# TensorE's share of two edge loops written as an engine loop, with buffer rings of four, eight and ten

## The reference

```python
# layer 0
edge_messages = relu(concat(x[dst], x[src], edge_attr, u[batch[dst]]) @ W1.T + b1)
aggregated    = segment_sum(edge_messages, dst)
x = layernorm(x + relu(concat(x, aggregated, u) @ W2.T + b2))
# layer 1
h          = relu(concat(x[row], x[col], edge_attr) @ msg_w1 + msg_b1)
messages   = h @ msg_w2 + msg_b2
aggregated = segment_sum(messages, col) / max(count, 1)
x = layernorm(x + (relu(concat(x, aggregated) @ upd_w1 + upd_b1) @ upd_w2 + upd_b2))
```

## Time and profile before

| | us |
|---|---|
| median of 3 runs | 4138.87 (4137.64 to 4140.2) |
| the profiled execution, its own time | 4140.49 |
| its span, first to last instruction | 4138.7 |
| first L615 of layer 0 to its last L598 | 98.28 to 2005.48 |
| first L615 of layer 1 to its last L598 | 2133.50 to 4044.41 |

### The profile page before, as it was taken

The page is one execution under the profiler, slowest core; times in us unless marked ns, Lnnn a source line. Parts: engine busy times, 40 slices in busy tenths (PEclk is TensorE's granted clock), DMA queues, the critical chain, the costliest instruction groups (busy, mean ns, idle before and its releaser), DMA issues. The chain is left out here.

```text
span 4138.7 us, 53825 instructions
## 1 busy us (share of the span) xinstructions
PE 3378.5 (82%) x16906; PEld 3171.1 (77%) x16906; DVE 1671.5 (40%) x3965; ACT 591.0 (14%) x1005; POOL 2981.5 (72%) x3156
## 2 busy tenths in 40 slices
PE   6998788877888888788779878878788787887886
PEld 4998787777878778787759877777777777777773
DVE  4544444444444444444445443434333333333333
ACT  1111111111111111111321111111111111111113
POOL 4777777777777777777267777777777777777772
PEclk6555555555555555555755555555555555555556
DMA  6554444444444444444155444444444444444431
GB/s 227 167 162 130 140 131 145 143 133 140 131 140 142 139 140 131 140 135 143 53 159 172 140 142 140 131 139 130 140 143 138 140 131 140 132 148 141 131 118 34
DMA packets 286577, 569.11 MB, mean 138 GB/s; under 512 B 165416, under 2 KB 197523, under 8 KB 248976
## 3 DMA queue, kind: packets, MB, share of 16 engines
q1 hardware_dynamic: 185326, 357.82, 25.7%
q0 software_dynamic: 100096, 205.20, 18.6%
q10 hardware_dynamic: 866, 2.56, 0.2%
HBM read 545.86 MB, written 19.45 MB: 137 GB/s over the span
## 5 line engine op out<-in xcount | busy, mean ns | idle before, releaser
L206 POOL DMA_INDIRECT Qr<-tabQ,srcE x3128 | 2960.7, 947 | 1074.7 <-issue 969.1
L615 PE MATMUL bank<-wall,BIG 128*128 128x128 f32 x6256 | 1596.3, 436 | 35.0 <-DMA BIG<-in_eaT 35.0
L628 PE MATMUL bank<-BIG 128*128 128x42 f32 x6256 | 1459.8, 413 | 13.0 <-ACT BIG L557 13.0
L615 PEld LDWEIGHTS bank<-wall,BIG 128*128 128x128 f32 x6256 | 1419.2, 331 | 35.4 <-DMA BIG<-in_eaT 35.4
L628 PEld LDWEIGHTS bank<-BIG 128*128 128x128 f32 x6256 | 1420.7, 331 | 13.6 <-ACT BIG L557 13.6
L587 DVE TENSOR_TENSOR BIG<-bank,Qr 128x512 f32<-128x512 f32 x782 | 539.6, 690 | 2097.9 <-issue 1727.3
L619 PE MATMUL bank<-BIG 126*128 126x128 bf16 x3128 | 484.1, 310 | 648.4 <-DVE BIG L570 647.8
L557 ACT ACTIVATE BIG<-BIG 128x512 f32<-128x512 f32 x782 | 492.4, 630 | 3364.1 <-DVE BIG L587 3364.1
L619 PEld LDWEIGHTS bank<-BIG 126*128 126x128 bf16 x3128 | 339.3, 141 | 774.8 <-DVE BIG L570 748.1
L570 DVE TENSOR_TENSOR BIG<-bank,BIG 126x512 bf16<-126x512 f32 x782 | 534.2, 683 | 34.3 <-DMA BIG<-in_dstR 34.0
L576 DVE TENSOR_TENSOR BIG<-bank,relE 128x168 f32<-128x168 f32 x782 | 251.5, 322 | 0.0
(11 more groups left out here) (94 smaller groups left out, 481.0 us busy)
## 6 DMA issues: line engine op xcount, KB each, us to landing
BIG<-in_eaT SPq DMA_DIRECT2D x196, 1024.0 KB, 5.6
BIG<-in_dstR SPq DMA_DIRECT2D x96, 1008.0 KB
Qr<-tabQ,srcE POOLq DMA_INDIRECT x3128, 2.5
BIG<-tabP SPq DMA_DIRECT2D x782, 31.5 KB
tabP<-BIG SPq DMA_DIRECT2D x24, 384.0 KB, 2.8
tabQ<-BIG SPq DMA_DIRECT2D x24, 256.0 KB, 4.0
X<-in_xN SPq DMA_DIRECT2D x1, 3136.0 KB, 12.0
out<-BIG SPq DMA_DIRECT2D x12, 256.0 KB, 2.3
```

What stands on the lines that cost most here:

```text
L206: e.indirect_dma_start(Q[:, g % R_Q, j, :], None, tabQ[l][:, :], bass.IndirectOffsetOnAxis(ap=srcE[:, g, j:j + 1], axis=0)).then_inc(es[l] ...
L615: e.matmul(bank[i % R_C][:, j * D:(j + 1) * D], ea[:, k % R_EA, (i % LQ * J + j) * P:(i % LQ * J + j + 1) * P], wc[l], start=(j == 0), sto ...
L628: last = e.matmul(bank[4 + g % 2][:, 0:W], M[:, g % R_M, j, :], S[:, g % R_S, j, :], start=(j == 0), stop=(j == J - 1))
```

## The change

TensorE's body becomes a function `group(i, t, dt)`. The first eight groups are written out as before, then a loop on the engine runs 47 turns of eight groups (groups 8 to 383) with the loop's register `t` from 1 to 47, and the last seven groups and the two trailing half turns are written out again. Inside the loop the slots of the rings are constants, so each ring that TensorE touches has to divide eight: `R_ST` goes from 3 to 4, `R_S` from 6 to 8, `R_M` from 3 to 4. Each wait's value is computed from `t`. `R_Q` goes from 12 to 10, and `PF`, which was `R_Q - 2`, is now `R_Q`, so that it stays 10. `BIG`, the area that holds the rings other than Q, grows from 11904 to 13072 words a partition. The other engines' code is unchanged but for the sizes of the rings.

```diff
-R_EA, R_PB, R_BC, R_Q, R_ST, R_S, R_M, R_PT = 2, 4, 2, 12, 3, 6, 3, 4
+R_EA, R_PB, R_BC, R_Q, R_ST, R_S, R_M, R_PT = 2, 4, 2, 10, 4, 8, 4, 4
+STEP = 8
-PF = R_Q - 2
-NBIG = 11904
+PF = R_Q
+NBIG = 13072
...
-                        for i in range(NG + 2):
-                            if i < NG:
+                        def group(i, t, dt):
+                            if dt + i < NG:
                                 k = i // LQ
                                 if i % LQ == 0:
-                                    e.wait_ge(v_ea[k % R_EA], 16 * (k // R_EA + 1))
-                                if i >= R_C:
-                                    e.wait_ge(v_tt, i - R_C + 1)
+                                    e.wait_ge(v_ea[k % R_EA], t * (16 * STEP // LQ // R_EA) + 16 * (k // R_EA + 1))
+                                if dt + i >= R_C:
+                                    e.wait_ge(v_tt, t * STEP + (i - R_C + 1))
...
-                                e.wait_ge(v_st, i + 1)
-                                e.wait_ge(v_pb[i % R_PB], 16 * (i // R_PB + 1))
+                                e.wait_ge(v_st, t * STEP + (i + 1))
+                                e.wait_ge(v_pb[i % R_PB], t * (16 * STEP // R_PB) + 16 * (i // R_PB + 1))
...
-                            if g >= 0:
-                                e.wait_ge(v_rl, g + 1)
-                                e.wait_ge(v_s, g + 1)
-                                if g >= 2:
-                                    e.wait_ge(v_ag, g - 1)
+                            if dt + g >= 0:
+                                e.wait_ge(v_rl, t * STEP + (g + 1))
+                                e.wait_ge(v_s, t * STEP + (g + 1))
+                                if dt + g >= 2:
+                                    e.wait_ge(v_ag, t * STEP + (g - 1))
...
-                                    e.wait_ge(v_cn, g + 1)
+                                    e.wait_ge(v_cn, t * STEP + (g + 1))
...
+                        for i in range(STEP):
+                            group(i, 0, 0)
+                        with e.Fori(1, NG // STEP) as t:
+                            for i in range(STEP):
+                                group(i, t, STEP)
+                        for i in range(NG // STEP * STEP, NG + 2):
+                            group(i, 0, 0)
```

## The result

The changed kernel takes 4154.81 us (median of 6 runs, 4152.76 to 4156.86) against 4138.77 us for the kernel before (6 runs, 4137.64 to 4141.1): 16.0 us more, a ratio of 1.0038 with a 95% interval of 1.0025 to 1.0051. The forecast was 17.6 us more.

A forecast was written before the change was run, and what follows sets the result against it. GpSimd's unbroken gathers were taken to bound both loops; 2 x (10.0 - 1.2) = 17.6 us added to the median of 4138.9 gave 4156.5 us, own range 4154 to 4160, eight in ten 4151 to 4168.

The forecast's parts named there:

- GpSimd bounds both loops: Both layers' loops: GpSimd's unbroken gathers need 5.00 us a group against TensorE's 4.02, so GpSimd sets each loop's end.
- Eight gathers per loop lose their head start: Start of each loop: with ten slots full, eight more gathers wait for the first sum, 10.0 us a loop, 20.0 together.
- The first load has less company: Start of each loop: without early gathers the first sum comes 1.2 us earlier, bounds 0 and 1.7.
- TensorE's loop costs nothing: TensorE's computed waits: 58 of 52 ns, 3.0 us a turn in layer 0, hidden by slack of 7.3 us a turn.
- The first rival: TensorE's loop: 165 ns exposed per computed wait makes TensorE the bound in layer 0, total 4274 us; chance 0.09.
- TensorE's waits on L570: Sign that the forecast is right: these waits of TensorE inside the loops shrink but stay.
- The body is fetched once: TensorE's jump back: fetching code anew costs nothing from below, 7.2 us a turn from above; nothing was taken.
- The rings of ST, S and M: Deeper rings let VectorE and ScalarE run further ahead inside the loops; price and gain nothing.
- The sum: Whole kernel: 17.6 us over the median of 4138.9, giving 4156.5 us, 0.43% slower.
- the second rival: Loops' gathers: GpSimd's step shrinks; 10 ns each gives 4126 us, faster than before from 5.8 ns on; chance 0.04.
- The two terms of the forecast: Loop starts: 10.0 us a loop for eight late gathers, less 1.2 us for an earlier first sum.

The follow-up runs named there:

- paced pair: Kernel before, and it with the changed rings, both taking two of four gathers plus memsets except in layer 0's first ring: 3976.20 and 3998.51 us.
- loop_q12: Changed kernel with Q's ring twelve instead of ten and S's ring four instead of eight: 5078.08 us, ratio 0.9993 to the kernel before; run again, 5139.51 us, 1.0066.
- loop_pf8: Changed kernel with eight instead of ten groups gathered ahead of each loop, Q's ring still ten: 5062.13 us, ratio 0.9966 to the kernel before.
- unrolled_rings: Kernel before with only the rings changed (Q ten with ten groups ahead, ST 4, S 8, M 4), TensorE's program unrolled: 5088.95 us, ratio 1.0011.
- half_loop: Changed kernel with only two of a group's four blocks of rows gathered from the eleventh group of each loop on: 3482.48 us.
- paced_before: Kernel before with two of four gathers replaced by three memsets each, in all groups but layer 0's first ring: 3976.20 us.
- half_unrolled: Changed kernel without TensorE's engine loop, only two of four blocks gathered from the eleventh group of each loop on: 3483.24 us.

## Why the prediction was right

- **GpSimd bounds both loops, at 5.00 us a group.** Right. After the change it waits on L588 at the two starts and otherwise keeps its gaps of 0.30, and the last gather of each loop carries the whole delay.
- **Eight gathers per loop lose their head start, 10.0 us each.** Right: the first gather of each loop ends a wait on the first sum, and the counts behind it are 1524. In the paced pair the same step gave two groups per loop, as worked out.
- **The first load has less company, 1.2 us a loop.** Right in kind and nearly in size: from the first load's issue to the first sum 1.36 us less in layer 0 and 1.04 in layer 1, bounds 0 and 1.7.
- **TensorE's loop costs nothing, at most 3.0 us a turn under the cover of its slack.** Right that it is nothing, and there is less to hide than I priced. I counted 58 computed waits of 52 ns; the values are shared, and the sequencer spends 0.5 us a turn on them and 0.2 on the jump. The cover was not even needed: with TensorE as the bound the pair differs by -0.8 us in 3482. The first rival falls. One sign of the forecast did not come: TensorE's waits on L570 (L571 now) were to shrink, from 647.8 us, and are 653.4 us (the weight loads' waits there did shrink, from 748.1 to 626.2).
- **The body is fetched once.** I left this between nothing and 7.2 us a turn. It is nothing: 18 blocks in all.
- **The rings of ST, S and M cost and gain nothing.** No row speaks against it; in the paced pair the loops are accounted for without them to 0.2 us, and the step inside them is the same.
- **The sum.** 17.6 us forecast, 16.0 measured; the loops of the profiled pair show 14.0. What the forecast did not have is a step of the gathers shorter by 1.4 ns in layer 0 and 0.8 ns in layer 1, 3.4 us in all. It goes the way of the second rival, at 1.1 ns on average a fifth of the 5.8 ns from which that would decide. It need not be the change's doing: one gather lasts 944 ns in the median in the changed kernel and 945 in the kernel before, but the same unrolled kernel with the changed rings shows 944, 944 and 947 on three chips, and `loop_q12` and `loop_pf8`, with TensorE's loop, 947. So an unrolled program, with all its code traffic, can have the shorter gather, and programs with the loop the longer one; what sets the two was not found. The two terms of the forecast come to 17.4 in the trace, 20.0 less 2.6 at the two starts; with the shorter step, 14.0 in the loops, and 12.3 for the whole spans. That the medians differ by 16.0, nearer to the forecast than the profiled pair does, is in part luck: the executions of either kernel scatter over 3.5 and 4.1 us.

## What to carry to other kernels

Find the engine that never waits, and ask of each edit what it does to the start of that engine's chain. A prefetch depth and a ring depth are two numbers. Here ten groups were gathered ahead in both kernels, and the ring alone, twelve or ten, set how many groups were under way when the first slot came free; taking memory from that ring to give it to others moved the end of each loop by whole steps. What the prefetch depth does to the time by itself no undisturbed run shows. An engine loop of 47 turns with some 340 matmul and load records a turn was free here even on a saturated TensorE, so its price was what it asked of the buffers.

## What the runs showed of the hardware

The same program took 4139 us on the first occasions and 5084 to 5109 us on the chips of the later ones, with the granted clock nearly the same (0.517 and 0.513) and the gather's step the same 1.25 us. There, while GpSimd issued gathers without a break, other engines stood still for 7 us (`unrolled_rings`, L598) to 24 us (`half_loop`, L181) at a time with no other engine's work outstanding, and in the stretch shown TensorE took 7.4 us for eight passes that take 2.06 otherwise. Halving the gathers, or spacing them with memsets, made it vanish from the loops (3482 and 3976 us, each kernel's runs within 8 us); ahead of the loops it stayed wherever the gathers stayed unbroken, and went in layer 1 of `paced_before`, where they were spaced. It is not the fetching of TensorE's code: the loop with its 18 blocks had it as much as the unrolled program with 142. What differs between those chips was not found.

A fully busy TensorE ran at its 1.2 GHz level: busy for 1400.00 of 1400 us in layer 1 (1900 to 3300 us), granted clock 0.50, in `half_loop` and `half_unrolled`. In layer 0's loop of the kernel before, the 2.4 GHz level shows only near the start: granted 0.97 in 108 to 120 us, after TensorE had stood still for 2.31 us up to 102.67 and then worked without a pause, and 0.62 in 120 to 130, where it was busy for 6.76 of the 10 us.
